# Rotary chains of the second half moved behind the third group's split, and the small experts' stage as one block

## The chip, the cores and the metric

The kernel runs on one core of a Trainium2 chip. The metric is device time in microseconds (us), the median of several runs. The engines are TensorE (PE in the rows, its weight loads PEld), VectorE (DVE), ScalarE (ACT), GpSimd (POOL) and SyncE (SP), which here only issues DMAs. "remote" in a row is a releaser that the profile does not match to an instruction.

## What is computed

x is 8 x 512 x 256 (4096 tokens of width 256, 16 heads of 16). Eight sublayers run one behind the other, each on a layer norm of x and added to x:

```python
x = x + _L0_attn_a_ref(_layernorm(x), ...)   # decay attention
x = x + _L0_ffn_ref(_layernorm(x), ...)      # small experts
x = x + _L0_attn_b_ref(_layernorm(x), ...)   # rope attention
x = x + _L0_ffn_ref(_layernorm(x), ...)      # small experts, the same weights
x = x + _L1_attn_a_ref(_layernorm(x), ...)   # causal, one head
x = x + _L1_ffn_ref(_layernorm(x), ...)      # experts with a capacity, F = 1024
x = x + _L1_attn_b_ref(_layernorm(x), ...)   # latent attention, rope
x = x + _L1_ffn_ref(_layernorm(x), ...)
```

The two parts that the change touches, cut to what matters:

```python
# rope attention (and the end of the latent one, whose q is x itself)
q = q * cos + rotate_half(q) * sin
k = k * cos + rotate_half(k) * sin
attn = softmax(einsum('bqhd,bkhd->bhqk', q, k) * DH ** -0.5)
# small experts: 8 experts of 256 x 256, one for each token
probs = softmax(x @ Wg + bg)                 # over 256 columns
idx = argmax(probs); p = probs[idx]; e_idx = idx % 8
out = relu(x @ We[e_idx] + be[e_idx]) * p
```

## The kernel before

hybrid_stack runs one function per sublayer. x stays in SBUF as X, 32 tiles of 128 tokens.

**Attention (mha_layer, from line 1112).** Its variants are called decay, rope and latent by the prefix of their tensors. A body of 64 steps runs for each of the 8 batches. Step s takes one head and one block of 128 keys. TensorE computes the transposed scores (exp_scores, L1479) into one of two banks, ACT takes the exponential (L1640, rope_probs), and TensorE multiplies it with the values (L1510). In the same step TensorE computes an ordinary score tile for a later group (max_scores, L1466, rope_scores_q) into one of A_RING = 3 banks, and VectorE reduces it to the rows' maxima (L1721, rope_mx). A group is 4 heads, 16 steps. The maxima of a group run from 28 to 13 steps ahead of its first exponential (SPAN), and SPLIT_BEFORE = -12 puts split_maxima, four small VectorE operations that split the maxima in three bf16 parts (L1746 is the third), at steps 4, 20, 36 and 52. "The third group's split" is the one at step 20. TensorE transposes the parts, ACT copies them, and the SP queue spreads them to rows of the query operand (max_rows).

Beside these steps the body prepares the next batch by fixed tables of steps: USES for the projections, transposes and outputs on TensorE, ROTATE_AT and MIDDLE_AT for the rotary chains. In rope and latent there are NCH = 4 chains per batch, in the order k0, q0, k1, q1, where 0 and 1 are halves of 8 heads. Each chain turns one 128x512 operand and splits it in three bf16 parts, which go through memory (rope_parts_dram) to the operands KS and QS:

- at ROTATE_AT[j], VectorE: rotate, a shuffle of the source to rope_sh and the product with the cosines to rope_fc (L1707)
- one step later, GpSimd: rotary_sums (product with the sines L1302, sum L1304) and first_part (cast L1313, difference L1315)
- at MIDDLE_AT[j], ACT: middle_part, a cast that waits for that difference
- at MIDDLE_AT[j] + 1, GpSimd: last_part, and then the SP queue: write_parts, three DMAs

The tables of rope, and of latent, are

```python
        ROTATE_AT, MIDDLE_AT = [6, 9, 14, 18], [13, 19, 25, 31]
        ROTATE_AT, MIDDLE_AT = [6, 7, 14, 15], [13, 19, 25, 31]
```

The SP queue issues write_parts, load_group (the operands of the next batch's groups, each waiting for the writes of its half) and max_rows in one fixed order of steps. The GpSimd operations of two chains share double buffers (j % 2), and rotate waits for the difference of the chain two before. In the prologue of a layer all four chains run on VectorE.

**Small experts (routed_layer, routed_experts).** A layer is four blocks, each begun when every engine has ended the one before:

```python
    routing(nc, g, ins, False, 0, load_weights)
    routing(nc, g, ins, False, 1, dispatch_first)
    experts_small(nc, g, 0, dispatch_second)
    experts_small(nc, g, 1, gather_first, results)
```

routing(half) takes 16 tiles in four quads: ACT normalises, TensorE turns and multiplies with the gate (L142), VectorE adds the bias (L244) and finds the maximum and its index (L256 copies the indices of a quad), ACT sums the exponentials; then some 22 small VectorE operations, each waiting for the one before, with two counting matmuls between them, give each token its slot and each expert tile its expert. dispatch scatters the 16 tiles of tokens to DRAM, sorted by expert, with 16 indirect DMAs of GpSimd (L345), one half beside the routing of the other or beside its experts. experts_small(half) then takes 24 tiles (EXPERT_TILES) through rings of RING = 8 buffers: the SP queue loads a tile, TensorE turns it, ACT copies, TensorE multiplies with its expert's weights (L420), VectorE adds the bias (L464, experts1x_y), the SP queue stores. In the last block GpSimd gathers the first half's results back (L496) beside the second half's tiles, and ACT and VectorE add them to x within its last 8 tiles. The gather of the second half's results belongs to the prologue of the next layer.

## Time and profile before

| | us |
|---|---|
| median of the runs | 3296.66 (3292.15 to 3298.2) |
| the profiled execution | 3302.95 |
| its span | 3301.2, mean granted TensorE clock 0.894 |
| PE busy | 2665.1 (81%) |
| DVE busy | 1944.9 (59%) |
| ACT busy | 1498.7 (45%) |
| POOL busy | 786.8 (24%) |
| one maximum, L1721 rope_mx, x512 | 0.685 |
| one exponential, L1640 rope_probs, x512 | 0.600 |
| write of parts in rope, issue to landing | 2.7 |
| load of an operand in rope, rope_KS | 4.1 |
| load of an operand in rope, rope_QS | 4.6 |

How to read it: the span is the time between the first and the last instruction of the profiled execution. Busy time counts an engine's work, not its waits. Busy shares of the whole span are means over stages with different limits, so the rows below go by stage. The granted clock is a share of TensorE's full speed. A row of the timeline is start, duration, engine, line, operation, output<-inputs with shapes, and in brackets the idle time of the engine just before it with what ended it.

### The profile page before, as it was taken

Reading aid. Unit: us, or ns where it says so; the run is one execution under the profiler, and the core shown is the slowest. Engines: PE = TensorE matmul, PEld = TensorE weight load, DVE = VectorE, ACT = ScalarE, POOL = GpSimd, SP = SyncE. Lnnn points to the kernel's source line nnn. Section 1 sums busy time; section 2 is a strip of 40 time slices with the busy share of each in tenths; the row PEclk is TensorE's granted clock in tenths of the full one; section 3 lists DMA queues with packets and bytes.
Section 4 is the critical chain, followed back from the end, with each engine's and each line's share of the span. In section 5 each row is a group of like instructions: output and inputs, shape, how many; then the busy total and the mean of one; then the engine's idle time right before and its main releaser. Section 6 shows DMA issues by size and latency. Waiting matters only on the chain. (4 is left out here: it accounts for less than half of the span.)

```text
span 3301.2 us, 40308 instructions
## 1 busy us (share of the span) xinstructions
PE 2665.1 (81%) x12988; PEld 1380.9 (42%) x12988; DVE 1944.9 (59%) x5001; ACT 1498.7 (45%) x2906; POOL 786.8 (24%) x742
## 2 busy tenths in 40 slices
PE   4869999995557999999555796998399999976993
PEld 2334444434442333333444565566133333344662
DVE  4858888874338888887433443111788888842112
ACT  2457767775224666667422431111166666641110
POOL 0323322301233223430123103000434333202003
PEclk7789999997777999999777895999599999986996
DMA  7655555521343322221134002231422332211223
GB/s 236 184 199 166 162 158 162 169 69 63 104 147 120 102 83 87 87 91 55 61 106 141 3 1 99 90 115 64 133 78 87 116 96 80 86 62 68 102 109 115
DMA packets 213575, 351.31 MB, mean 106 GB/s; under 512 B 21192, under 2 KB 168265, under 8 KB 208632
## 3 DMA queue, kind: packets, MB, share of 16 engines
q1 hardware_dynamic: 197864, 299.06, 28.6%
q0 software_dynamic: 15504, 49.68, 4.6%
q8 instruction: 107, 1.75, 0.2%
q14 instruction: 100, 0.82, 0.1%
HBM read 203.24 MB, written 154.80 MB: 108 GB/s over the span
## 5 line engine op out<-in xcount | busy, mean ns | idle before, releaser
L1718 DVE CUSTOM_DVE_ANT_0 decay_junk<-decay_scores_q,decay_corr 128x512 bf16<-128x512 f32 x512 | 338.5, 685 | 118.0 <-PE decay_scores_q L1466 116.3
L1640 ACT ACTIVATE decay_probs<-decay_scores_k 128x512 f32<-128x512 f32 x512 | 294.7, 597 | 206.5 <-PE decay_scores_k L1485 170.3
L1721 DVE TENSOR_REDUCE rope_mx<-rope_scores_q 128x1 f32<-128x512 f32 x512 | 332.6, 685 | 87.5 <-PE rope_scores_q L1466 86.6
L1640 ACT ACTIVATE rope_probs<-rope_scores_k 128x512 f32<-128x512 f32 x512 | 295.0, 600 | 185.7 <-PE rope_scores_k L1479 184.9
L1640 ACT ACTIVATE latent_probs<-latent_scores_k 128x512 f32<-128x512 f32 x512 | 295.1, 600 | 180.2 <-PE latent_scores_k L1479 178.4
L1721 DVE TENSOR_REDUCE latent_mx<-latent_scores_q 128x1 f32<-128x512 f32 x512 | 329.3, 683 | 73.3 <-PE latent_scores_q L1466 73.1
L1466 PE MATMUL latent_scores_q<-latent_KS,latent_QS 96*128 96x512 bf16 x512 | 201.6, 396 | 63.5 <-DVE latent_mx L1721 47.3
L1466 PE MATMUL decay_scores_q<-decay_KS,decay_QS 96*128 96x512 bf16 x512 | 205.4, 402 | 46.9 <-DVE decay_mx L1718 35.1
L1466 PE MATMUL rope_scores_q<-rope_KS,rope_QS 96*128 96x512 bf16 x512 | 201.4, 395 | 27.3 <-DVE rope_mx L1721 18.4
L1479 PE MATMUL rope_scores_k<-rope_QS,rope_KS 99*128 99x512 bf16 x512 | 197.2, 387 | 9.7 <-ACT rope_probs L1640 7.6
L1479 PE MATMUL latent_scores_k<-latent_QS,latent_KS 99*128 99x512 bf16 x512 | 197.2, 387 | 8.1 <-ACT latent_probs L1640 5.6
L1482 PE MATMUL decay_scores_k<-decay_QS,decay_KS 99*128 99x384 bf16 (+3 forms) x512 | 156.7, 307 | 30.4 <-DMA decay_QS<-decay_mT 22.6
L1510 PE MATMUL decay_out_heads<-decay_probs,decay_Vaug 128*32 128x512 f32 x1024 | 139.1, 616 | 0.8 <-DVE decay_probs L1730 0.8
L1510 PE MATMUL latent_out_heads<-latent_probs,latent_Vaug 128*32 128x512 f32 x1024 | 137.1, 608 | 0.7 <-ACT latent_probs L1640 0.7
L1510 PE MATMUL rope_out_heads<-rope_probs,rope_Vaug 128*32 128x512 f32 x1024 | 136.4, 605 | 0.7 <-ACT rope_probs L1640 0.7
L1313 POOL CAST decay_parts<-decay_fc 128x512 bf16<-128x512 f32 x56 | 34.2, 611 | 405.8 <-DVE decay_fc L1704 381.8
L1482 PEld LDWEIGHTS decay_scores_k<-decay_QS,decay_KS 99*128 99x128 bf16 x512 | 49.4, 97 | 190.1 <-issue 82.3
L1479 PEld LDWEIGHTS rope_scores_k<-rope_QS,rope_KS 99*128 99x128 bf16 x512 | 49.1, 97 | 187.7 <-ACT rope_probs L1640 154.1
L496 POOL DMA_INDIRECT experts_XN<-cap_results,experts_back x64 | 63.1, 985 | 263.2 <-DMA cap_results<-experts4x_y 244.1
L1479 PEld LDWEIGHTS latent_scores_k<-latent_QS,latent_KS 99*128 99x128 bf16 x512 | 49.2, 97 | 179.1 <-ACT latent_probs L1640 135.1
L686 PE MATMUL experts4x_inner<-experts4x_xT,experts4x_w 128*128 128x512 f32 x256 | 114.3, 605 | 0.8 <-ACT experts4x_xT L737 0.8
L686 PE MATMUL experts3x_inner<-experts3x_xT,experts3x_w 128*128 128x512 f32 x256 | 113.9, 604 | 0.8 <-ACT experts3x_xT L737 0.8
(449 smaller groups left out, 5304.1 us busy)
## 6 DMA issues: line engine op xcount, KB each, us to landing
decay_parts_dram<-decay_parts SPq DMA_DIRECT2D x64, 384.0 KB, 3.0
decay_KS<-decay_parts_dram SPq DMA_DIRECT2D x64, 384.0 KB, 6.2
decay_QS<-decay_parts_dram SPq DMA_DIRECT2D x64, 384.0 KB, 6.9
decay_parts_dram<-decay_parts SPq DMA_DIRECT2D x64, 256.0 KB, 3.1
experts3x_w<-in_w_dram SPq DMA_DIRECT2D x16, 1024.0 KB, 7.3
experts4x_w<-in_w_dram SPq DMA_DIRECT2D x16, 1024.0 KB, 7.7
rope_parts_dram<-rope_parts SPq DMA_DIRECT2D x32, 384.0 KB, 2.7
rope_KS<-rope_parts_dram SPq DMA_DIRECT2D x32, 384.0 KB, 4.1
```

The lines of the kernel that those rows point to most:

```text
L496: pool.indirect_dma_start(out=g["XN"][:, i, :], out_offset=None, in_=ye, in_offset=bass.IndirectOffsetOnAxis(ap=g["back"][:, i:i + 1], axi ...
L686: last = pe.matmul(psH[:, f % 2, :], w1[:, p, c, f * P:(f + 1) * P], xT[:, p, c, :], start=(c == 0), stop=(c == 1))
L1313: eng.tensor_copy(parts[:, (nb * NCH + j) % RING, 0, :], fc[:, j % 2, :]).then_inc(p0_done, 1)
L1466: pe.matmul(psA[:, A_BANK[k], :], QS[0:96, 0, c, hh, qt * P:(qt + 1) * P], KS[0:96, NV - 1, c, hh, :], start=True, stop=True).then_inc(a_r ...
L1479: last = pe.matmul(psB[:, s % 2, :], KS[:, 0, c, hh, keys], QS[:, 0, c, hh, :], start=True, stop=True)
L1482: last = pe.matmul(psB[:, s % 2, 0:end], KS[:, 1, c, hh, keys], QS[:, 0, c, hh, 0:end], start=True, stop=True)
L1510: last = pe.matmul(psO[32 * h:32 * h + 32, :], Vaug[:, b % 2, kt, 4 * grp + h, :], probs[:, (b * 16 + kk) % PSLOTS, h, :], start=(kt == 0) ...
L1640: act.activation(probs[:, (b * 16 + kk) % PSLOTS, h, :], psB[:, s % 2, :], ACT.Exp, scale=scale).then_inc(exp_done, 1)
L1718: dve.tensor_tensor_reduce(junk[:, a % 2, :], psA[:, A_BANK[k], :], corr[:, qt, :], 1.0, -3.0e38, ALU.mult, ALU.max, mx[:, grp % 2, qt, h: ...
L1721: dve.tensor_reduce(mx[:, grp % 2, qt, h:h + 1], psA[:, A_BANK[k], :], AX.X, ALU.max).then_inc(a_done, 1)
```

## The change

In mha_layer, for rope and latent: chains 2 and 3 rotate at steps 21 and 24, where rope had 14 and 18 and latent 14 and 15 (chain 1 of latent at 8 instead of 7). ACT's cast of chain 1 stands at 17 instead of 19, of chain 2 at 28 instead of 25, of chain 3 at 32 instead of 31. The shuffle stays at ROTATE_AT, the product comes one step later, and the GpSimd part one step later again. decay keeps its order.

In the small experts' layers: the four blocks become one function, routed_small, with one block. Each engine runs through both halves of the routing and then all 48 tiles, and only semaphores order them. TensorE's counting matmuls of the first half stand behind the scores of the fifth quad. The operations for the slots come first, then slots_ready is raised, and those for the tiles' experts follow. GpSimd dispatches each half when its slots are ready, and gathers when tile 24's stores are done. The SP queue waits for all transfers of a half's dispatch ahead of that half's first load. The ring of 8 buffers runs through the 48 tiles. The expert weights are asked for by GpSimd ahead of everything. Slot and return index are the same tensor for these layers, so one copy goes.

```diff
-        ROTATE_AT, MIDDLE_AT = [6, 9, 14, 18], [13, 19, 25, 31]
+        ROTATE_AT, MIDDLE_AT = [6, 9, 21, 24], [13, 17, 28, 32]
...
-        ROTATE_AT, MIDDLE_AT = [6, 7, 14, 15], [13, 19, 25, 31]
+        ROTATE_AT, MIDDLE_AT = [6, 8, 21, 24], [13, 17, 28, 32]
...
+    SUMS_LATER = 1 if decay else 2
...
+            def products(j):
+
+                src = turned_from(j)[1]
+                dve.tensor_tensor(fc[:, j % 2, :], src, tab[:, 0 if not decay else CHAINS[j][2], :], ALU.mult).then_inc(rot_done, 1)
...
                 else:
                     dve.stream_shuffle(sh[:, j % 2, :], src, [i ^ 8 for i in range(32)]).then_inc(rot_done, 1)
-                    dve.tensor_tensor(fc[:, j % 2, :], src, tab[:, 0, :], ALU.mult).then_inc(rot_done, 1)
...
                             if ROTATE_AT[j] == s:
                                 rotate(tag, b, b + 1, j)
+                            if not decay and ROTATE_AT[j] + 1 == s:
+                                products(j)
...
-                            if ROTATE_AT[j] + 1 == s:
+                            if ROTATE_AT[j] + SUMS_LATER == s:
                                 rotary_sums(pool, b + 1, j)
                                 first_part(pool, b + 1, j)
...
+def routed_small(nc, g, ins, results):
...
+        @block.gpsimd
+        def _(pool):
+            pool.dma_start(we[:, :, :], ins["we"]).then_inc(loaded, 16)
+            pool.dma_start(be[:, :], ins["be"]).then_inc(loaded, 16)
+            pool.wait_ge(g["cleared"], 16 * CLEARS)
+            for h in range(2):
+                pool.wait_ge(slots_ready, h + 1)
+                dispatch(pool, g, xe[h], range(HALF_TILES * h, HALF_TILES * h + HALF_TILES), scattered[h])
+            for r in range(RING):
+                pool.wait_ge(y_stored[r], 16 * (EXPERT_TILES // RING))
+            for q in range(NB // 2):
+                results.gather(pool, q)
...
+            def load(n):
+                half, rows = place(n)
+                if n % EXPERT_TILES == 0:
+                    sp.wait_ge(scattered[half], 16 * HALF_TILES)
+                if n >= RING:
+                    sp.wait_ge(t_ready, n - RING + 1)
+                sp.dma_start(xin[:, n % RING, :], xe[half][rows, :]).then_inc(x_loaded[n % RING], 16)
...
+            for n in range(RING):
+                load(n)
+            for n in range(TILES):
+                store(n)
+                if n + RING < TILES:
+                    load(n + RING)
...
+            pe.wait_ge(gate_loaded, 32)
+            turn_normal(0)
+            for q in range(1, NQ):
+                turn_normal(q)
+                score(q - 1)
+                if q == NQ // 2 + 1:
+                    count(0)
+            score(NQ - 1)
+            pe.wait_ge(l_taken, 2 * NQ)
+            count(1)
+            pe.wait_ge(loaded, 32)
+            turn(0)
+            for ring in range(TILES // RING):
+                pe.wait_ge(te_ready, ring * RING // EXPERT_TILES + 1)
...
+                    if n + 1 < TILES:
+                        turn(n + 1)
+                    expert(n, at[r])
...
+            for q in range(NQ):
+                if q + 2 < NQ:
+                    normalise(q + 2)
+                if q + 1 < NQ:
+                    take_normal(q + 1)
+                exps(q)
+            for n in range(TILES):
+                take(n)
+                if n >= TILES - RING and n % 2 == 0:
+                    results.scale(act, n % RING // 2)
...
+                link(dve.tensor_reduce(rank[:, :], rk[:, :, :], AX.X, ALU.add))
+                dve.tensor_copy(slot[:, ts], rank[:, :]).then_inc(slots_ready, 1)
...
+                dve.tensor_copy(te[h][:, :], tef[:, :]).then_inc(te_ready, 1)
...
+            for h in range(2):
+                for q in range(h * NQ // 2, (h + 1) * NQ // 2):
+                    top_logits(q)
+                slots(h)
...
-    routing(nc, g, ins, False, 0, load_weights)
-    routing(nc, g, ins, False, 1, dispatch_first)
-    experts_small(nc, g, 0, dispatch_second)
...
-    experts_small(nc, g, 1, gather_first, results)
```

## Rows read from the trace of the kernel before

**Rows 1.** Windows by stage: stretch, busy time per engine (instructions), clock, DMA share, GB/s

```profile
764.00:972.00 208.00, 116.81 (x484) 92.79 (x484) 83.22 (x300) 68.57 (x180) 48.10 (x51) 0.76 0.33 109
1030.00:1572.00 542.00, 519.70 (x2708) 194.77 (x2706) 432.34 (x864) 362.73 (x671) 155.48 (x140) 1.00 0.27 83
1585.00:1796.00 211.00, 117.45 (x484) 92.89 (x484) 83.22 (x300) 68.73 (x180) 47.79 (x50) 0.75 0.33 107
2396.00:2926.00 530.00, 497.88 (x2653) 185.26 (x2651) 429.91 (x889) 356.81 (x657) 174.05 (x146) 0.99 0.27 85
```

**Rows 2.** The product's line: durations in ns, min/median/max, first and last start

```profile
L1707 DVE TENSOR_TENSOR rope_fc<-rope_f,rope_tab x32: 671/901/1629, 982.5 to 1472.3; 128x512 f32<-128x512 f32 x32
```

**Rows 3.** Timeline of VectorE in rope, around the third group's split

```profile
1258.04 1.87 DVE L1721 TENSOR_REDUCE rope_mx<-rope_scores_q 128x1 f32<-128x512 f32 x3
...
1261.65 1.63 DVE L1707 TENSOR_TENSOR rope_fc<-rope_f,rope_tab 128x512 f32<-128x512 f32 x1
...
1264.90 1.13 DVE L1746 CAST rope_mp<-rope_mr 128x16 bf16<-128x16 f32 x1
```

**Rows 4.** Timeline of GpSimd in the same stretch

```profile
1263.36 1.27 POOL L1302 TENSOR_TENSOR rope_sh<-rope_sh,rope_tab 128x512 f32<-128x512 f32 x1 [0.63 <-DVE rope_fc L1707]
1264.71 1.29 POOL L1304 TENSOR_TENSOR rope_fc<-rope_fc,rope_sh 128x512 f32<-128x512 f32 x1
...
1266.80 1.16 POOL L1315 TENSOR_TENSOR rope_rr<-rope_fc,rope_parts 128x512 f32<-128x512 f32 x1
```

**Rows 5.** Timeline of TensorE in the same batch

```profile
1266.90 0.39 PE L1466 MATMUL rope_scores_q<-rope_KS,rope_QS 96*128 96x512 bf16 x1 [0.67 <-DVE rope_mx L1721]
...
1277.37 0.38 PE L1466 MATMUL rope_scores_q<-rope_KS,rope_QS 96*128 96x512 bf16 x1
1278.14 0.39 PE L1479 MATMUL rope_scores_k<-rope_QS,rope_KS 99*128 99x512 bf16 x1 [0.40 <-ACT rope_probs L1640]
```

**Rows 6.** Timeline of TensorE in latent, at the third group's split

```profile
2623.53 0.38 PE L1479 MATMUL latent_scores_k<-latent_QS,latent_KS 99*128 99x512 bf16 x1
2625.36 0.39 PE L1466 MATMUL latent_scores_q<-latent_KS,latent_QS 96*128 96x512 bf16 x1 [1.45 <-DVE latent_mx L1721]
```

**Rows 7.** Windows: steps 18 to 24, 34 to 40 (rope), 16 to 24, 32 to 40 (latent)

```profile
1260.19:1267.97 7.78, 6.77 (x39) 1.95 (x38) 7.42 (x14) 5.34 (x11) 6.79 (x8) 1.00 0.06 20
1278.57:1285.04 6.47, 6.44 (x39) 2.21 (x39) 5.29 (x14) 4.36 (x10) 0.25 (x1) 1.00 0.83 258
2616.68:2626.43 9.75, 7.69 (x43) 2.19 (x41) 9.07 (x17) 6.33 (x13) 9.38 (x9) 1.00 0.23 82
2635.94:2643.49 7.55, 7.12 (x42) 2.32 (x41) 6.37 (x15) 5.44 (x11) 1.16 (x1) 1.00 1.00 324
```

**Rows 8.** Timeline of VectorE, first layer of small experts

```profile
800.07 0.17 DVE L256 COPY experts1r_first<-experts1r_idx 128x4 uint32<-128x4 uint32 x1
...
820.52 0.69 DVE L244 TENSOR_TENSOR experts1r_lg<-experts1r_logits,experts_bg 128x512 f32<-128x512 f32 x1 [12.74 <-PE experts1r_logits L142]
...
832.09 0.69 DVE L244 TENSOR_TENSOR experts1r_lg<-experts1r_logits,experts_bg 128x512 f32<-128x512 f32 x1 [6.43 <-remote]
...
847.23 0.17 DVE L256 COPY experts1r_first<-experts1r_idx 128x4 uint32<-128x4 uint32 x1
...
863.44 0.42 DVE L464 TENSOR_TENSOR experts1x_y<-experts1x_results,experts_be 128x256 f32<-128x256 f32 x1 [8.50 <-PE experts1x_results L420]
...
933.21 0.42 DVE L464 TENSOR_TENSOR experts1x_y<-experts1x_results,experts_be 128x256 f32<-128x256 f32 x1 [7.37 <-remote]
```

**Rows 9.** Timeline of GpSimd, first of each burst of 16 indirect transfers

```profile
809.17 1.07 POOL L345 DMA_INDIRECT dispatched<-experts_XN,experts_slot  x1 [43.10 <-SPq L59]
...
856.14 0.97 POOL L345 DMA_INDIRECT dispatched<-experts_XN,experts_slot  x1 [26.66 <-POOLq L59]
...
911.77 1.00 POOL L496 DMA_INDIRECT experts_XN<-results,experts_back  x1 [35.45 <-POOLq L354]
```

**Rows 10.** Timeline of ACT, first instruction of the layer behind

```profile
971.66 1.28 ACT L1562 ACT_TABLE_LOAD   x1 [6.93 <-PEq L354]
```

More of the change, by code:

```diff
@@ L45, with dispatch @@
 RANK_TILES = 8
-def routing(nc, g, ins, capacity, half=0, alongside=None):
-    t0, nt = half * HALF_TILES, HALF_TILES
-    X, MV, RSTD, XN = g["X"], g["MV"], g["RSTD"], g["XN"]
-    ident, con = g["ident"], g["con"]
-    slot, back, weight = (g[n][:, t0:t0 + nt] for n in ("slot", "back", "weight"))
-    te, wg, bg, nmr, loaded = g["te"][half], g["wg"], g["bg"], g["nmr"], g["gate_loaded"]
-    LP = 1 if capacity else 2
-    NQ = nt // 4
+def dispatch(pool, g, xe, tiles, scattered):
+    for i in tiles:
+        pool.indirect_dma_start(out=xe, out_offset=bass.IndirectOffsetOnAxis(ap=g["slot"][:, i:i + 1], axis=0),
+                                in_=g["XN"][:, i, :], in_offset=None, bounds_check=xe.shape[0] - 1,
+                                oob_is_err=False).then_inc(scattered, 16)
@@ new lines, in store @@
+            def store(n):
+                half, rows = place(n)
+                sp.wait_ge(y_taken, n + 1)
+                sp.dma_start(ye[half][rows, :], y[:, n % RING, :]).then_inc(y_stored[n % RING], 16)
+            for n in range(RING):
[4 more added lines that the diff above has]
+                    load(n + RING)
+            for r in range(RING):
+                sp.wait_ge(y_stored[r], 16 * (TILES // RING))
@@ L147, in _ @@
[L147 to L158 removed]
+                            last = pe.matmul(psL[:, n % 4, t * D:(t + 1) * D], xnT[:, q % 2, c, tok:tok + P], wg[:, c, :],
+                                             start=(c == 0), stop=(c == 1))
@@ new lines, in score, with count @@
+                    last.then_inc(l_ready, 1)
+            def count(h):
+                pe.wait_ge(oh_ready, h + 1)
+                flat = ohb[:, :, :].rearrange("p t e -> p (t e)")
+                pe.matmul(psR[:, :, :].rearrange("p t e -> p (t e)"), g["before"][:, :], flat, start=True,
+                          stop=True).then_inc(counted, 1)
+                pe.matmul(psC[:, :, :].rearrange("p t e -> p (t e)"), g["ones"][:, :], flat, start=True,
+                          stop=True).then_inc(counted, 1)
@@ new lines, in normalise, with take_normal @@
+            def normalise(q):
+                for i in range(4 * q, 4 * q + 4):
+                    act.activation(XN[:, i, :], X[:, i, :], ACT.Identity, bias=nmr[:, i:i + 1],
+                                   scale=RSTD[:, 0, i:i + 1]).then_inc(xn_ready, 1)
+            def take_normal(q):
+                for c in range(2):
+                    act.wait_ge(n_ready, 2 * q + (c + 1))
+                    if c == 0 and q >= 2:
+                        act.wait_ge(l_ready, 2 * q - 2)
+                    act.copy(xnT[:, q % 2, c, :], psT[:, c, :]).then_inc(n_taken, 1)
@@ L192, in pair @@
-            def pair(j):
-                normalise(j * 2 + 2)
-                take(j * 2 + 1, 1)
-                exps(j * 2, 0)
-                normalise(j * 2 + 3)
-                take(j * 2 + 2, 0)
-                exps(j * 2 + 1, 1)
-            if not capacity and not half:
-                act.wait_ge(rstd_done, 2)
+                    act.activation(ex[:, t % 2, :], lg[:, i // 2 % 4, t % 2, :], ACT.Exp, bias=ntop[:, i:i + 1],
+                                   accum_out=sums[:, i:i + 1]).then_inc(exp_done, 1)
@@ L481 @@
+            for ring in range(TILES // RING):
+                dve.wait_ge(te_ready, ring * RING // EXPERT_TILES + 1)
+                at = tile_experts(mybir.EngineType.DVE, ring)
+                for r in range(RING):
+                    n = ring * RING + r
+                    result(n, at[r])
+                    if n >= TILES - RING and r % 2 == 1:
+                        results.add(dve, r // 2, st)
 class Results:
```

493 lines of the change are left out of this document (148 added, 345 removed).

## The prediction

> **What bounds the kernel now.** I read the mean busy shares by stage first. In the rope and latent stretches (542 and 530 us) TensorE is busy 519.7 and 497.9 us at full clock and VectorE 432 and 430 us [rows 1]. So TensorE sets the pace there, and a microsecond saved anywhere else counts only where TensorE stands idle for it. In the two stretches of the small experts (208 and 211 us) no engine is busy for much more than half of the time: TensorE 117 us, VectorE 83, ACT 69, GpSimd 48 [rows 1]. Those stages are bound by the order of waits and by the boundaries between blocks. I therefore cost the first part of the change by TensorE's idle spots, and the second by the chain from stage to stage. The page's chain of waits is of no use, as it covers the tail alone.
>
> **Part 1, the rotary chains.** One chain is a shuffle and a product on VectorE, then four GpSimd operations, then a cast on ACT, then one more GpSimd operation and the writes by the SP queue. There are four chains per batch, for batches 1 to 7, so seven times per layer. A product alone takes 0.67 us, its median in rope is 0.90 and the longest 1.63 [rows 2]. The long ones start while GpSimd is in an elementwise operation. The product at 1261.65 took 1.63 us. The cast of the third group's split at 1264.90, 128x16 and nothing more, took 1.13 us [rows 3], and it ended with the GpSimd product that had started at 1264.71 and ran 1.29 us [rows 4]. Behind that cast stand the fourth split operation and the maxima, and TensorE waits for the maxima: the scores at 1266.90 come after 0.67 us of idleness, with VectorE named as releaser [rows 5]. In latent the same place costs more: 1.83 us lie between the matmul at 2623.53 and the next at 2625.36 [rows 6], where 0.22 is usual in both layers.
>
> The Trainium skill, page "SBUF — State Buffer", section "SBUF: two separate sides", says that GpSimd and those VectorE operations that read two SBUF inputs or use both ports share an exclusive lock, and whoever starts first keeps it for the whole instruction. The trace agrees in the three long operations above. The rule speaks for the change at the split, where GpSimd falls silent, and against it at step 25, where the fourth product now lands in the third chain's GpSimd work. By the rule that product waits for at most one GpSimd operation.
>
> What moves: chains 2 and 3 go from steps 14 and 18 (rope; 14 and 15 latent) to 21 and 24, each product one step later, each GpSimd start one later again, and the ACT cast of chain 1 from 19 to 17, of chain 2 from 25 to 28, of chain 3 from 31 to 32. Nothing is added or removed. The gain is read from a twin. Steps 34 to 40 hold the same TensorE work as steps 18 to 24 (39 matmuls each), without rotation. The rope stretch takes 7.78 us at 18 to 24 and 6.47 at 34 to 40, so 1.31. In latent, steps 16 to 24 take 9.75 against 7.55 at 32 to 40, so 2.20, with one matmul more [rows 7]. A second idle spot goes with the ACT cast of chain 3. At step 31 it delays the exponential that TensorE needs next, 0.77 us from 1277.37 to 1278.14 instead of 0.22 [rows 5], so 0.55. At step 32 the delay falls behind the value sums of step 34 and is hidden. That makes 1.86 at most in rope and, with some 0.2 for a small gap at step 16, 2.95 in latent. I take 1.7 and 2.9. Times seven: 12 + 20 = **32 us**.
>
> What is late next. VectorE, counted from step 20 with maxima at 0.6 us (three in 1.87 [rows 3]): split 0.8, shuffle 0.65, heads 0.7, product 0.65, shuffle 0.7, product 0.7 to 1.9. It falls about 3 us behind, and TensorE may run three score banks ahead, so I find no wait of TensorE at steps 25 to 29. GpSimd starts chain 2 some 4.5 us after step 20 and needs 4.6 us per chain (1263.36 to the end of the operation at 1266.80 [rows 4]), so chain 3's remainder is ready 13.9 us after step 20. ACT wants it at step 32, 13.5 us after step 20, but does an exponential of 0.6 first. That margin is 0.2 us: if GpSimd is slower by 1.3 us, ACT stands 1.1 us in each of 14 batches, with the exponentials and so TensorE queued behind it. The SP queue gets chain 3's writes about 16 us after step 20 instead of 15, and behind them the load of the next batch's group 1. With 1.5 us to issue the writes and the page's 4.6 to land the load, it is there at about 25, with what else stands in the queue; step 52 needs it at about 33 (13.5 plus 20 steps of about 1 us, as 512 steps take some 542 us [rows 1]). Bounds of this part: 16 us (half of it kept, ACT late at step 32) and 44 (3 per batch).
>
> **Part 2, the small experts as one block**, counted in the first of the two layers and taken twice. Four blocks become one, so three boundaries go in each layer.
> Second half's logits. VectorE adds the second half's first logits at 820.52, after 12.74 us of idleness behind the first slot chain [rows 8], as ACT, TensorE and VectorE start again from an empty pipe. In one block, TensorE and ACT have two quads ready. The new slot chain starts at 800.2, behind the last small copy of the first half at 800.07 [rows 8], takes the 7 us that it takes now (VectorE went idle at 807.8, which is 820.52 less 12.74), and waits some 2.5 us (an estimate, the scores of a quad less what VectorE does meanwhile) for the counting matmuls, which now stand behind the scores of quad 4, so VectorE goes on at about 809.2: 11.3 us saved. The quads themselves take 5.05 us each (15.14 for the three from 832.09 to 847.23 [rows 8]). That added queueing does not delay the first dispatch: it started at 809.17 [rows 9] and can start at 808, since four small operations now come behind the slots and no boundary.
> The stall. At 832.09 VectorE had waited 6.43 us for something that the profile names "remote" [rows 8], and at 933.21 again, 7.37 us. Both fall in the second half of a burst of 16 indirect transfers by GpSimd, started at 809.17 and 911.77 [rows 9], of some 20 us at about 1.3 from one to the next, and end some 2 us behind it. The first half's tiles have a stall of the same kind and length in the burst from 856.14. The bursts stay. I take the first stall as half kept: the last quad ends at 834 (829.7 without, 836.1 with), against 847.3.
> Second slot chain: the ids of the tile experts now come behind the slots, and no boundary follows. Dispatch follows the last quad by 6 us instead of 8.9, so it starts at 840, **16 us** earlier.
> First tiles: before, the first result came 7.3 us after the dispatch burst began (863.44 against 856.14). Now TensorE turns tile 0 while VectorE is in the slot chain, and the result comes 1.7 us after. The stall that ends with the burst takes a part back: four results had come by 21.4 us (933.21 is the fourth of its half, its burst began at 911.77), now nine, and those five tiles are worth some 1.1 us each at the full clock. So **6 us**, bounds 0 and 13.
> Boundary between the halves: the gather started at 911.77 and the layer after it at 971.66 [rows 10], 60 us. Tiles of the second half no longer wait for the first half's last store and a boundary, 10 us in all, and reach their own stall with about six more tiles done. The end comes 49 us after the gather: **11 us**, bounds 7 and 19.
> Sum 33 us a layer, bounds 20 (three stalls whole, first tiles nothing) and 51 (no stalls). Twice: **66 us**, bounds 40 and 102. The waits added (GpSimd for slots and for the stores of 24 tiles; the SP queue for the dispatch ahead of tile 24's load, with stores 17 on queued behind it) come due later than what they wait for by this reckoning: the second dispatch is done at about 860, and tile 16 is stored at about 874.
>
> **The rivals.**
> A: the stalls belong to the bursts wholly and the rotation gives half. Experts 20 a layer, rotation 16: 56 us, 3241. For it: all stalls end with a burst. Against: in the first half of each burst work runs normally.
> B: the stalls belong to the restarts (an empty pipe and code just entered) and vanish with them. Experts 51 a layer, rotation 40: 142 us, 3155. For it: the one at 933.21 strikes at the fourth tile after a restart. Against: the one at 832.09 is far from a restart.
> C: the rotation gives nothing because ACT stands at step 32 for chain 3; experts 66: 3231.
> D, slower: the SP queue is one line. If chain 3 reached it over 7 us later than reckoned, the load of group 1 would miss step 52, and each us beyond costs 14. At 15 us late that is 112 us lost against 66 gained, 3343. The margin of 7 us speaks against it.
>
> **How the numbers follow.** The profiled execution took 3302.95 us, span 3301.2; the median of the runs is 3296.66, so 6.3 below. 3302.95 less 98 is 3205, and on the scale of the median **3199**. Own range of this case 3175 to 3222, chance 0.50. A 0.20, B 0.17, C 0.09, D 0.03; 0.01 for anything else. A measurement of this kernel can tell about 0.2% (6.6 us) from no change. Range 3160 to 3243: it takes in A and C, and most of what lies between the forecast and B, and leaves out the ends of B and D. Chances: faster 0.94, same 0.02, slower 0.04.
>
> **What would show it.** Rotation: the split's cast at step 20 takes 0.17 us, not 1.13; TensorE's idle time on VectorE's maxima at steps 19 to 24 is gone; the rope stretch takes about 530 us where 542 stand in [rows 1], the latent one about 510 instead of 530. Wrong if ACT stands ahead of the cast of chain 3. Experts: VectorE's idle time ahead of the fifth quad is under 1 us, the second dispatch starts 16 us earlier against the layer's start, and a layer takes about 175 us instead of 208. Wrong if the waits named "remote" grow, or if GpSimd's gather no longer ends before the last eight tiles need it.

## The result

The changed kernel takes 3215.94 us (median, 3212.75 to 3217.52) beside 3297.43 us for the kernel before in the same comparison. The ratio is 0.9747, with an interval of 0.9732 to 0.9762: 81.5 us or 2.5% faster. The forecast was 3199 with a range of 3160 to 3243. The profiled execution took 3217.11 us, 85.8 less than the one of before (3302.95).

The page of the changed kernel, its first part (busy us, share of the span, instructions):

```profile
span 3215.4 us, 40264 instructions
## 1 busy us (share of the span) xinstructions
PE 2644.4 (82%) x12988; PEld 1373.2 (43%) x12988; DVE 1911.3 (59%) x4987; ACT 1497.1 (47%) x2906; POOL 784.3 (24%) x742
```

TensorE, ACT and GpSimd have nearly the work that they had. VectorE is busy 33.6 us less (1911.3 instead of 1944.9), of which 30.9 lie in the rope and latent windows. The rest of the gain is idle time that went. The windows of the changed kernel (columns as in [rows 1]) are first rope, latent and the two experts' layers whole, then steps 18 to 24 in rope and 16 to 24 in latent, the last step included, as in the first and the third row of [rows 7]:

```profile
1010.00:1538.00 528.00, 515.94 (x2713) 195.41 (x2714) 414.66 (x865) 363.17 (x672) 156.94 (x140) 0.99 0.28 85
2335.00:2842.00 507.00, 491.62 (x2657) 184.90 (x2659) 416.68 (x889) 357.23 (x658) 170.34 (x146) 0.99 0.28 89
767.70:952.30 184.60, 110.00 (x484) 87.62 (x484) 81.76 (x293) 67.55 (x180) 47.70 (x51) 0.79 0.38 122
1550.40:1733.10 182.70, 110.68 (x484) 87.83 (x484) 81.69 (x293) 67.43 (x180) 47.68 (x50) 0.79 0.38 124
1234.02:1240.09 6.07, 6.03 (x38) 1.99 (x31) 5.09 (x14) 4.87 (x10) 1.16 (x1) 1.00 0.58 199
2545.34:2552.89 7.55, 7.43 (x43) 2.28 (x42) 6.46 (x16) 6.34 (x13) 3.46 (x4) 1.00 0.59 208
```

The whole span by layer, each from the start of ACT's first table load in it to that of the next layer. The first two columns are the pair above; the next two are the same two kernels on another chip, and the last the block alone on a third chip (all from the experiments below):

| layer, us | before | after | before, 2nd chip | after, 2nd chip | block alone, 3rd chip |
|---|---|---|---|---|---|
| start and decay | 764.4 | 767.7 | 764.5 | 771.9 | 772.9 |
| small experts, first | 207.2 | 184.5 | 175.5 | 154.5 | 154.1 |
| rope | 613.6 | 598.1 | 616.6 | 598.3 | 615.3 |
| small experts, second | 210.2 | 182.7 | 177.4 | 151.5 | 152.4 |
| causal and its experts | 511.1 | 512.8 | 505.7 | 506.3 | 505.9 |
| latent | 633.0 | 608.1 | 628.4 | 603.9 | 625.1 |
| last experts | 361.7 | 361.4 | 360.0 | 360.1 | 360.2 |

In the pair the two experts' layers gave 22.7 and 27.5 us, rope 15.5 and latent 24.9, 90.6 in all. Layers that the change doesn't touch took 4.8 us more, 3.3 of it ahead of the first experts' layer. That stretch varied from 763.3 to 772.9 us over the traces, whatever the kernel, so it belongs to no part of the change. A batch of rope, from its first exponential to that of the next, went from 70.23 to 68.20 us, and one of latent from 68.32 to 65.07.

The rope batch of [rows 3 to 5] in the changed kernel (timelines; product's line first, as in [rows 2]):

```profile
L1545 DVE TENSOR_TENSOR rope_fc<-rope_f,rope_tab x32: 671/681/903, 963.1 to 1447.4; 128x512 f32<-128x512 f32 x32
```

```profile
1236.99 0.17 DVE L1596 CAST rope_mp<-rope_mr 128x16 bf16<-128x16 f32 x1
...
1242.78 0.89 DVE L1545 TENSOR_TENSOR rope_fc<-rope_f,rope_tab 128x512 f32<-128x512 f32 x1
...
1241.85 1.28 POOL L1147 TENSOR_TENSOR rope_fc<-rope_fc,rope_sh 128x512 f32<-128x512 f32 x1
1243.18 0.95 POOL L1156 CAST rope_parts<-rope_fc 128x512 bf16<-128x512 f32 x1
...
1248.72 1.16 POOL L1158 TENSOR_TENSOR rope_rr<-rope_fc,rope_parts 128x512 f32<-128x512 f32 x1
...
1249.91 0.62 ACT L1450 CAST rope_parts<-rope_rr 128x512 bf16<-128x512 f32 x1 [0.44 <-POOL rope_rr L1158]
...
1249.02 0.39 PE L1322 MATMUL rope_scores_k<-rope_QS,rope_KS 99*128 99x512 bf16 x1
1249.25 0.38 PE L1309 MATMUL rope_scores_q<-rope_KS,rope_QS 96*128 96x512 bf16 x1
1249.52 0.39 PE L1322 MATMUL rope_scores_k<-rope_QS,rope_KS 99*128 99x512 bf16 x1
```

The split's cast takes 0.17 us where it took 1.13, and the median product 0.68 instead of 0.90. This holds for every batch: before, the third group's cast took 1.13 us in six batches of rope and 1.02 in six of latent; after, it takes 0.17 or 0.18 in all sixteen. At the end of [rows 5] TensorE waits for ACT and 0.77 us lie between two starts; here they are 0.27 (1249.25 to 1249.52), where 0.22 is usual.

The first experts' layer in the changed kernel (timelines of VectorE, GpSimd and ACT), to be held against [rows 8 to 10]:

```profile
811.88 0.68 DVE L293 TENSOR_TENSOR experts_lg<-experts_logits_results,experts_bg 128x512 f32<-128x512 f32 x1
...
828.79 0.69 DVE L293 TENSOR_TENSOR experts_lg<-experts_logits_results,experts_bg 128x512 f32<-128x512 f32 x1 [6.72 <-PE experts_logits_results L175]
...
834.43 0.69 DVE L293 TENSOR_TENSOR experts_lg<-experts_logits_results,experts_bg 128x512 f32<-128x512 f32 x1 [3.13 <-DMA con_sb<-in_con_dram]
...
842.04 0.17 DVE L305 COPY experts_first<-experts_idx 128x4 uint32<-128x4 uint32 x1
...
896.23 0.42 DVE L340 TENSOR_TENSOR experts_y<-experts_logits_results,experts_be 128x256 f32<-128x256 f32 x1 [0.66 <-PE experts_logits_results L200]
899.51 0.42 DVE L340 TENSOR_TENSOR experts_y<-experts_logits_results,experts_be 128x256 f32<-128x256 f32 x1 [2.85 <-PE experts_logits_results L200]
...
922.16 0.42 DVE L340 TENSOR_TENSOR experts_y<-experts_logits_results,experts_be 128x256 f32<-128x256 f32 x1 [10.12 <-remote]
...
848.17 0.97 POOL L51 DMA_INDIRECT dispatched<-experts_XN,experts_slot  x1 [16.05 <-DVE experts_slot L329]
...
952.26 1.28 ACT L1405 ACT_TABLE_LOAD   x1 [6.94 <-PEq L61]
```

VectorE goes on with the second half's logits without an idle spot (811.88), and then stands 6.72 and 3.13 us for the two signals of TensorE on that half's third quad (quad 6, counted from 0), and later 10.12 us for something "remote". The releaser of the 3.13 us, a load of constants, had long been done: the semaphore that came last is TensorE's.

From the start of each layer, the milestones of the first experts' layer on both chips:

| us from the layer's start | before | after | before, 2nd chip | after, 2nd chip |
|---|---|---|---|---|
| second half's first logits | 56.1 | 44.2 | 56.8 | 44.2 |
| last quad's indices | 82.8 | 74.3 | 77.9 | 67.5 |
| second dispatch begins | 91.7 | 80.4 | 86.8 | 73.7 |
| first half's last result | 144.0 | 128.5 | 125.2 | 110.8 |
| second half's first result | 154.2 | 131.8 | 135.4 | 114.2 |
| layer's end | 207.2 | 184.5 | 175.5 | 154.5 |

### The profile page after: what moved, and what is told of

Read it like the earlier page. It is cut to its first block and busy times, and to the rows that moved or that the text cites. A ratio compares the mean times of both kernels' runs of the same rounds, so it can differ in the third digit from the quotient of the medians.

```text
span 3215.4 us, 40264 instructions
## 1 busy us (share of the span) xinstructions
PE 2644.4 (82%) x12988; PEld 1373.2 (43%) x12988; DVE 1911.3 (59%) x4987; ACT 1497.1 (47%) x2906; POOL 784.3 (24%) x742
## 5 line engine op out<-in xcount | busy, mean ns | idle before, releaser
L1571 DVE TENSOR_REDUCE latent_mx<-latent_scores_q 128x1 f32<-128x512 f32 x512 | 330.3, 684 | 67.1 <-PE latent_scores_q L1309 66.7
L1483 ACT ACTIVATE latent_probs<-latent_scores_k 128x512 f32<-128x512 f32 x512 | 294.9, 600 | 151.5 <-PE latent_scores_k L1322 149.8
L200 PE MATMUL experts_logits_results<-experts_we,experts_xT 128*128 x384 | 118.7, 439 | 48.1 <-issue 29.3
L340 DVE TENSOR_TENSOR experts_y<-experts_logits_results,experts_be 128x256 f32<-128x256 f32 x96 | 39.7, 424 | 142.7 <-PE experts_logits_results L200 86.0
```

The source lines that it names most:

```text
L200: last = pe.matmul(psL[:, n % 2, 0:D], xT[:, n % 2, c, :], we[:, c, bass.ds(at, D)], start=(c == 0), stop=(c == 1))
L340: dve.tensor_tensor(y[:, n % RING, :], psL[:, n % 2, 0:D], be[:, bass.ds(at, D)], ALU.add).then_inc(y_taken, 1)
L1483: act.activation(probs[:, (b * 16 + kk) % PSLOTS, h, :], psB[:, s % 2, :], ACT.Exp, scale=scale).then_inc(exp_done, 1)
L1571: dve.tensor_reduce(mx[:, grp % 2, qt, h:h + 1], psA[:, A_BANK[k], :], AX.X, ALU.max).then_inc(a_done, 1)
```

## The experiments

All experiments start from the changed kernel, but for the one run of the kernel before. They ran on three chips, none of them the pair's; the kernel before took 3227 to 3231 us on each, 67 to 70 less than in the pair.

**The block alone.** The old tables, product with the shuffle, sums one step later:

```diff
-        ROTATE_AT, MIDDLE_AT = [6, 9, 21, 24], [13, 17, 28, 32]
+        ROTATE_AT, MIDDLE_AT = [6, 9, 14, 18], [13, 19, 25, 31]
...
-        ROTATE_AT, MIDDLE_AT = [6, 8, 21, 24], [13, 17, 28, 32]
+        ROTATE_AT, MIDDLE_AT = [6, 7, 14, 15], [13, 19, 25, 31]
...
-    SUMS_LATER = 1 if decay else 2
+    SUMS_LATER = 1
...
-                            if not decay and ROTATE_AT[j] + 1 == s:
+                            if not decay and ROTATE_AT[j] == s:
```

> The changed kernel with the old tables of steps, the product in the same step as the shuffle and the sums one step later: the small experts' block alone. By stages, the trace after shows 23 and 27 us gained in the two experts' layers and 15 and 25 us in the rope and latent layers. Theory: the two parts are independent, so this kernel takes 3216 + 40 = 3256 us, 41 below the kernel before. Rival: a part of the rope and latent gain comes from the block (code, buffers or queues left in another state by the layer before): then under 3245.

Measured: 3177.21 us beside 3227.03, ratio 0.9840 (0.9824 to 0.9856), 50 below the kernel before. Scaled to the pair that is 3245 us, just the bound that the rival had been given, so the total alone doesn't decide. The expected 41 had been reckoned back from the medians (81.5 less 40), while the stages of the same pair say 50. The stages decide it: rope took 615.3 us and its batches 70.22, as before. In latent most batches kept their 68.32. Two longer batches that the kernel before shows on the second chip (69.52 us in the sixth, 69.07 instead of 67.46 in the seventh) were not there, which is 2.8 us; in the pair only the first of the two stands (69.54), 1.2 us. With the 21.0 and 25.9 us that the experts' layers give on the second chip, that makes the 50. So the block leaves the rope batches alone and takes at most 3 us from latent. The rotary change without the block was not run.

**Shuffle and product in one step**, with the new tables:

```diff
-    SUMS_LATER = 1 if decay else 2
+    SUMS_LATER = 1
...
-                            if not decay and ROTATE_AT[j] + 1 == s:
+                            if not decay and ROTATE_AT[j] == s:
```

> The changed kernel with the new tables, but shuffle and product in one step and the GpSimd sums one step later, as before. Theory: the gain comes from the tables (TensorE's waits at the split are gone because GpSimd is silent there), and the two steps add nothing, since TensorE has three score banks of slack: 3216 within 3. Rival: 1.4 us of VectorE work in a row instead of two times 0.7 shows at TensorE, in 28 chains of each of two layers at 0.2 us: 3227. With the sums a step earlier, chain 3's cast on ACT at step 32 could only find its input earlier, so no loss is expected there.

Measured: ratio 0.9740 (0.9724 to 0.9756), 3143.0 us. A batch of rope takes 68.64 us instead of 68.20 and one of latent 65.51 instead of 65.07, on this chip too (the next kernel has the unchanged tables there). So the two steps are worth 0.44 us a batch, 6 us of the 40. They are worth it at steps 25 to 31, which take 9.25 us here and 8.78 in the changed kernel; steps 16 to 24 take the same in both (8.50 in rope, 7.55 in latent). The rival's mechanism is real at half its size, and the tables carry the rest.

**A pause after 8 of 16 indirect transfers** in both dispatches and the gather:

```diff
+                for part in range(2):
+                    if part:
+                        pool.wait_ge(scattered[h], 16 * 8)
...
+                if q == 2:
+                    pool.wait_ge(results.gathered[0], 64)
+                    pool.wait_ge(results.gathered[1], 64)
```

> The changed kernel; within the experts' block GpSimd waits after 8 of the 16 indirect transfers of a burst until all 8 have landed (both dispatches and the gather). Theory 1: TensorE's late signals come from a backlog that a long burst builds up, so with bursts of 8 the waits of VectorE on them (10, 9 and 14 us in the first layer) mostly go, at 3 us more per burst: 3216 less 15 to 35. Theory 2: they come with every indirect transfer that TensorE's work meets: the same waits stay, and the pauses cost 0 to 10 us more. Theory 3: they come from code entered for the first time: unchanged, 3216.

Measured: ratio 0.9725 (0.9709 to 0.9741), 3137.32 us, experts' layers 153.7 and 151.3 us. The question could not be put: in the experts' layers this chip showed no wait "remote" and no late signal, in any kernel, pause or not.

**Plain transfers in place of the indirect ones:**

```diff
-                dispatch(pool, g, xe[h], range(HALF_TILES * h, HALF_TILES * h + HALF_TILES), scattered[h])
+                for i in range(HALF_TILES):
+                    pool.dma_start(xe[h][i * P:(i + 1) * P, :], g["XN"][:, HALF_TILES * h + i, :]).then_inc(scattered[h], 16)
```

> The changed kernel; in the experts' block the 16 indirect transfers of each dispatch and of the gather are plain transfers of the same tiles by the same engine, so the tokens are not sorted and the results are not put back in order (the index part is left out). Theory 1, indirect bursts hold TensorE's signals up: VectorE's long waits on TensorE vanish in both halves, each experts' layer takes 35 us less, and the whole about 3216 - 60 = 3156. Theory 3, first entry of code or restarts: the waits stay, and only the 20 us of issue per dispatch shrink; 3190 or more.

Measured: ratio 0.9737 (0.9720 to 0.9753), 3141.94 us, experts' layers 153.4 and 150.5. This kernel leaves the sorting out. The 16 plain transfers are issued in 8.5 us, where 16 indirect ones take some 20, and yet the layers are within about a microsecond of those with indirect transfers (154.5 and 151.5, 153.5 and 151.9). Where TensorE's signals are on time, the longer issue of a burst costs nothing that these runs can tell.

**Both kernels unchanged on one more chip**, to have traces side by side. 

> The kernel before, unchanged, for a trace on the same chip as the kernels beside it. On the chip of the first experiments it took 3227 us, 70 less than in the pair on record, and the changed block's layer took 154 us there instead of 184. Theory: the late signals of TensorE in the experts' layers (waits of VectorE of 6 and 7 us, called remote) differ from chip to chip and not from kernel to kernel; where they are missing, each of this kernel's experts' layers takes 207 - 28 = 179 us or so, and no wait on remote stands in them. Rival: this kernel has them on every chip and only the one block can lose them: then 207 here beside 154.

> The changed kernel, unchanged, for a trace and an interval on the same chip. Theory: ratio as on record, 0.9747, within 0.003 on either kind of chip, since the late signals cost both kernels about the same. Rival: on a chip without them the block gains more, 50 us a layer as in rival B of the prediction: ratio 0.957.

Measured: the kernel before 3229.72 us; the changed one 3138.06, ratio 0.9715 (0.9702 to 0.9728). The waits of VectorE in the first experts' layer of the kernel before on this chip:

```profile
DVE experts1x_y L464 <- PE experts1x_results L420: 58.0, 42, 9.7
DVE experts1r_lg L244 <- PE experts1r_logits L142: 27.5, 4, 12.8
```

and of the changed kernel there:

```profile
DVE experts_y L340 <- PE experts_logits_results L200: 45.1, 40, 4.4
DVE experts_lg L293 <- PE experts_logits_results L175: 17.1, 3, 11.5
DVE experts_y L340 <- issue: 3.3, 1, 3.3
```

Columns: waited in total, times, longest. No "remote" in either. By the layer table the kernel before is 31.7 and 32.8 us longer in these layers on the pair's chip, the changed one 30.0 and 31.2. By the milestones of the first layer nearly all of it lies in the stretches that hold a burst: the way to the last quad's indices and the tiles of each half (4.9, 13.9 and 12.9 us in the kernel before; 6.8, 11.0 and 12.4 in the changed one). So the late signals strike both kernels alike, on the one chip that shows them, and the block gains nearly the same with them (22.7 and 27.5) as without (21.0 and 25.9). Rival B of the prediction falls: the stalls didn't vanish with the restarts.

The ratio is 0.9715 where 0.9747 within 0.003 was expected. It misses that bound by a hair, the two intervals don't touch, and the gain by medians is 92.7 us instead of 81.5. It is still far from the rival's 0.957. The profiled executions, of which this one is the slowest of five of the changed kernel (3148.09), give 81.6 us, so the traces can't say where the other 11 lie.

**ACT's cast of chain 3 at step 31 in rope, at 33 in latent:**

```diff
-        ROTATE_AT, MIDDLE_AT = [6, 9, 21, 24], [13, 17, 28, 32]
+        ROTATE_AT, MIDDLE_AT = [6, 9, 21, 24], [13, 17, 28, 31]
...
-        ROTATE_AT, MIDDLE_AT = [6, 8, 21, 24], [13, 17, 28, 32]
+        ROTATE_AT, MIDDLE_AT = [6, 8, 21, 24], [13, 17, 28, 33]
```

> The changed kernel with ACT's cast of chain 3 at step 31 in rope and at step 33 in latent, instead of 32 in both. The trace after has the chain's difference ready 13.8 us after step 20 (13.9 in the prediction), and ACT stands 0.45 us for it at step 32. Theory: at step 31 ACT stands 0.9 us, the exponential of step 32 is that late, and rope's batch of 68.2 us becomes 69.0 (6 us in the layer); at step 33 ACT does not stand, and latent's 65.07 stays, as the 0.45 lay behind the value sums. Rival: slack in the score banks hides the wait at 31 too, and rope stays at 68.2; or the wait at 32 does cost, and latent falls to 64.7.

Measured: 3153.99 us, ratio 0.9770 (0.9755 to 0.9785), 16 us above the changed kernel, all of it in rope (614.4 us). Latent stays at 65.05 a batch: the 0.44 us at step 32 are hidden. Rope's batches became 69.7 to 71.3, 2.4 more on the mean where 0.8 was expected. The timelines of TensorE and ACT in the fourth batch:

```profile
1221.58 0.39 PE L1322 MATMUL rope_scores_k<-rope_QS,rope_KS 99*128 99x512 bf16 x1 [1.44 <-ACT rope_probs L1483]
...
1220.41 0.62 ACT L1450 CAST rope_parts<-rope_rr 128x512 bf16<-128x512 f32 x1 [0.93 <-POOL rope_rr L1158]
```

ACT stands the 0.93 us that were expected. The exponential of step 32 then comes behind wait and cast both, 1.5 us late, and TensorE stands 1.44. Steps 25 to 31 take 10.32 us instead of 8.78, and in the batches of 71 us steps 32 to 40 take 8.8 instead of 7.56 as well. So one step in a table costs 2.4 us a batch, more than the whole second idle spot was priced at (0.55).

**ACT ahead, with the pause:**

```diff
+                if q == NQ // 2:
+                    normalise(q + 3)
+                    take_normal(q + 2)
                 exps(q)
```

> The changed kernel with the pause after 8 indirect transfers of the earlier experiment, and ACT's normalising and copies of quads 6 and 7 ahead of the exponentials of quad 4, which wait for the first slot chain. In the trace after VectorE waits 6.7 us for the logits of quad 6, of which 3 come from that order on ACT and the rest from TensorE's late signal. Theory: 3 us less per layer, so 6 below the changed kernel, on either kind of chip. On a chip with late signals the pause tells whether they come from the length of a burst: then 15 to 35 less in all; if not, the remote waits stand in this trace too.

Measured: 3133.30 us, ratio 0.9701 (0.9686 to 0.9716). On the same chip the changed kernel has 3138.06. The last quad's indices come 64.7 us after the first experts' layer's start, where the kernels with the old order have 67.1 to 67.5 on these chips, and VectorE's wait of 3.07 us for quad 6 is gone. So the order on ACT gives its 3 us at that place. Whether the layer keeps them is not shown. The layers take 150.7 and 149.4 us, 3.8 and 2.1 less than in the changed kernel's trace, but the kernel of the experiment before, which has the old order, took 150.2 and 149.7 on the same chip. The medians differ by 4.8 us, and the intervals of the two ratios overlap.

**The experts' numbers read without a check of bounds:**

```diff
-                                                                 max_val=(E - 1) * D)
+                                                                 max_val=(E - 1) * D,
+                                                                 skip_runtime_bounds_check_because="clamped to E - 1")
```

> The changed kernel; the experts of 8 tiles are read into registers without the check of their bounds (the values are clamped before). The trace of the changed kernel shows at every 8th tile a load of 0.8 us and then, for each of 8 values, an operation and an assertion, 0.28 us for both, on TensorE and VectorE: 3.3 us between results instead of 1.1. This was left out of the prediction, which took the whole 10 us between the halves' tiles as boundary. Theory: it is work of TensorE's sequencer, so 8 x 0.28 = 2.2 us go at each of 6 rings, 13 a layer: 26 below the changed kernel (3112 where that takes 3138, ratio to the kernel before 0.963). Rival: the gap at a ring is the wait for the tile's load or store, and the reading lies beside it: under 6 us in all.

Measured: 3112.74 us, ratio 0.9627 (0.9605 to 0.9648), the value expected; experts' layers 136.5 and 136.5. VectorE's waits for the results in the first experts' layer, where the changed kernel has 45.1 us, the longest 4.4:

```profile
DVE experts_y L341 <- PE experts_logits_results L201: 29.9, 40, 1.5
```

TensorE's waits on nothing but its own queue in the same layer, in the changed kernel (on the second chip) and then in this one:

```profile
PE experts_turned L192 <- issue: 11.7, 5, 2.8
```

```profile
PE experts_turned L193 <- issue: 0.8, 2, 0.6
```

The gap between the halves' results is now 1.5 us (1.1 in the second layer) where the changed kernel has 3.3, and 1.1 is usual between two tiles. Most of the gap was the reading.

**Both**, without the pause: 

> The same, with ACT's work for quads 6 and 7 ahead of the exponentials of quad 4 as in the earlier experiment. Theory: the two lie one behind the other in the layer and add: 6 us below the kernel without that order, 32 below the changed one, ratio 0.961. Rival: the second dispatch's 20 us of issue end the wait for the second half's tiles once the first half's are quicker, so that the 6 us are not seen twice: 29.

Measured: 3107.58 us, ratio 0.9617 (0.9599 to 0.9635), experts' layers 135.0 and 134.1. That is 3.9 us less in the two layers than without the check alone, and 5.2 less by medians, where 6 were expected. The intervals of the two ratios overlap, so these runs can't tell 3 from 6, nor either surely from nothing. It is the best kernel of the study: 1.0% below the changed one, by ratios to the kernel before.

**Both, with the pause:** 

> The same again with the pause after 8 indirect transfers. On a chip where VectorE's waits on late signals of TensorE are missing: within 3 us of the kernel without the pause, as before. On a chip that has them: if they come from the length of a burst, this kernel alone loses them, 15 to 60 us; if not, its trace has them like the others.

Measured: 3118.68 us, ratio 0.9655 (0.9637 to 0.9672), experts' layers 140.6 and 139.9. That is 11 us above the kernel without the pause, where 3 at most were expected. Again no late signals on this chip. The pause, which cost nothing that can be seen in the changed kernel, costs 5.7 us a layer once the tiles are quicker. It is lost behind the start of the gather: from there to the layer's last result 26.3 us pass without the pause and 30.8 with it (first layer).

## Why the prediction came out as it did

The sum was 98 us and the profiled pair gave 85.8. Two misses of opposite sign stand in it, so part of the closeness is luck: the rotary part gave 8.4 us more than reckoned, the experts' part 15.8 less, and the layers that nobody touched took 4.8 more. By steps:

- **Rotary chains: 32 expected, 40.4 measured** (rope 12 and 15.5, latent 20 and 24.9). The mechanism is shown. The cast at the split fell from 1.13 to 0.17 us, and steps 16 to 24 of latent fell by 2.20 us, to the 7.55 of the twin exactly. In rope steps 18 to 24 fell by 1.71 where the twin gave 1.31, but the window's start had moved: ACT's exponential of step 18 comes 0.4 us later against step 16. From step 16 on, the fall is 1.32, the twin's value. The second idle spot was priced too low, 0.55 where steps 25 to 31 gave 0.74 in rope and 0.75 in latent (0.47 of it hangs on the product's step of its own, by the second experiment), and the small gap at step 16 of latent, taken as 0.2, gave 0.32 (17.76 us to that step before, 17.44 after). Windows of rope's fourth batch, steps 16 to 24, 25 to 31 and 32 to 40, first in the kernel before, then in the changed one (columns as in [rows 1]):

```profile
1258.15:1267.97 9.82, 8.68 (x51) 3.02 (x49) 9.19 (x17) 7.37 (x14) 8.70 (x9) 1.00 0.23 80
1267.97:1277.49 9.52, 9.48 (x49) 4.58 (x48) 6.04 (x11) 6.48 (x13) 2.26 (x2) 1.00 0.66 196
1277.49:1285.04 7.55, 7.12 (x42) 2.32 (x41) 6.37 (x15) 5.44 (x12) 1.15 (x1) 1.00 0.86 275
1231.59:1240.09 8.50, 8.34 (x51) 3.21 (x50) 6.65 (x16) 7.29 (x14) 1.58 (x2) 1.00 0.54 185
1240.09:1248.87 8.78, 8.78 (x47) 4.35 (x45) 7.04 (x13) 6.01 (x12) 7.92 (x8) 1.00 0.31 91
1248.87:1256.43 7.56, 7.53 (x43) 2.41 (x43) 6.78 (x16) 5.95 (x12) 3.23 (x3) 1.00 0.61 201
```

  A batch gave 2.03 us in rope and 3.25 in latent; 1.7 and 2.9 had been taken out of caution from 1.86 and 2.95. The first batch, not counted apart, gave 3.1 and 3.4. Of latent's gain 1.2 us in the pair, up to 3 on the second chip, may come with the block, by the first experiment.
- **What is late next: right.** The chain's difference was to be ready 13.9 us after step 20. It was ready at 1249.88, 13.8 us after (step 20 begins at 1236.12). ACT stood 0.44 us at step 32. The prediction had called that a sign of being wrong, and it came, but TensorE didn't feel it: with the cast at step 33 latent's batches stay the same. Rival C had the right place and a margin as thin as stated: one step earlier costs 16 us. The SP queue (rival D) was on time: it asked for group 1's operands at 1254.99, 18.9 us after step 20, and with 4.6 to land they are there at about 24, where 25 was reckoned.
- **The lock.** The Trainium skill, page "SBUF — State Buffer", section "SBUF: two separate sides", was read as a product that waits for at most one GpSimd operation. The fourth product took 0.89 us beside the sum that ran to 1243.13, and the GpSimd cast at 1243.18 took 0.95 instead of its median 0.61, being still under way when the product ended at 1243.67. The trace agrees with an exclusion in both directions to within 0.15 us (a full wait would have made 1.02 of the product). It costs 0.2 us on VectorE and 0.3 on GpSimd, in the fourth chain; the median product (0.68) meets none. The prediction calls the operation at 1264.71 in [rows 4] GpSimd's product; it is the sum (L1304), and the reading of the wait is the same.
- **Second half's logits: 11.3 expected, 11.9 measured.** No fault in the mechanism. The terms given (800.2, 7 and 2.5) add up to 809.7 and not to 809.2, so the sum should have been 10.8.
- **The stall: this step failed.** It was taken as half kept, so the last quad was to end at 834 (half between 829.7 and 836.1 is 832.9, a slip of 1.1 us), which is 69.6 us from the layer's start. It ended at 74.3. VectorE stood 9.9 us (6.72 and 3.13) instead of 6.43. About 3 of these are no stall: ACT had the copy of quad 6 for TensorE behind the exponentials of quad 4, which wait for the slot chain, an order that stands in the diff and was overlooked. On the second chip, without late signals, that wait is 3.07 us, and the experiments that turned the order round have it no more. The rest was kept whole. The dispatch does follow the last quad by the 6 us that were reckoned (6.1), but it came 11.3 us earlier instead of 16.
- **First tiles: 6 expected, 4.2 measured** (15.5 at the last result of the first half, less 11.3). Inside its bounds of 0 and 13. The first result came 3.9 us after the dispatch began and not 1.7, as VectorE reads the first eight experts' numbers there too (1.5 without the check), and six results had come by 21.4 us instead of nine.
- **Boundary between the halves: 11 expected, 7.2 measured.** The 10 us between the halves' results were counted as boundary. They were 10.2 before and are 3.3 now, because every eighth tile pays for reading the next eight experts' numbers. The trace of before showed this inside one block, between its eighth and its ninth result, and it was not looked at. The experiment without the check takes most of it away. From the gather's start to the layer's end 52.1 us pass, where 49 were reckoned. The rows of the kernel before (timeline of VectorE), 3.06 us from start to start where 1.08 is usual:

```profile
885.64 0.42 DVE L464 TENSOR_TENSOR experts1x_y<-experts1x_results,experts_be 128x256 f32<-128x256 f32 x1 [1.40 <-PE experts1x_results L420]
888.70 0.76 DVE L464 TENSOR_TENSOR experts1x_y<-experts1x_results,experts_be 128x256 f32<-128x256 f32 x2 [2.63 <-PE experts1x_results L420]
```

- **Sum of the experts' part: 66 expected, 50.2 measured**, inside its bounds of 40 and 102. The second layer gave 4.8 more than the first because its first quads had been 5 us slower before (40.5 us to the fourth quad instead of 35.6) and were not after.
- **The range held.** The result lies between the forecast and rival A (3241), whose first half came true (stalls kept whole) and whose second didn't (rotation gave more, not half). The waits named "remote" grew in length too (VectorE's longest in the first layer is 10.12 us, before it was 7.37), the prediction's sign of being wrong for the experts' part, which did come out below its forecast.

What stays open: why TensorE's signals to VectorE come late on one chip and not on three others, with the same program and the same bursts. The traces show them late only within bursts of indirect transfers and up to some 3 us behind a burst's last issue. In the changed kernel one of them is nearly 8 us late (quad 6's second signal, given with the matmul at 826.49, let VectorE go at 834.43). The layers are about 30 us longer for it in both kernels, by the comparison of chips. No run with altered bursts met a chip that shows it, so neither the length of a burst nor its kind was tested.

## What to carry to other kernels

A twin stretch of the same loop, with the same work and without the suspect, prices an interference well: 1.31 and 2.20 us reckoned, 1.32 and 2.20 found, once the windows begin at the same kind of step. When a boundary is taken out, look for what of its idle time stands inside the blocks too (here reading registers at every eighth tile), since that stays. And when blocks are joined, read each engine's new order for work that now stands behind a wait of another chain.

## What was not expected of the hardware

A read of 8 values from SBUF into registers, with a check of bounds on each, held TensorE and VectorE for about 2 us more than without the check: 96 tiles in rings of 8 gave 28 us back, 0.9% of the kernel (0.9715 on one chip, 0.9627 on another). Chips differ: the same two kernels ran 67 and 78 us quicker on the second chip by their medians, 2.0% and 2.4%, and in the profiled executions 65 and 61 us of that lie in the two experts' layers. The ratio moved by 0.003 (0.9747 and 0.9715), which is beyond the noise of either, so a gain carries better from chip to chip than a time does, but not exactly.
